# Halving the last adjacency piece block by block in steps 4 to 9, with the x batches' work shifted by a step, in a float32 graph-layer kernel

## The reference

```python
h = jnp.maximum(_layernorm(x, axis=-1), 0.0)      # x: 8192 x 128, float32
support = jnp.matmul(h, W)                        # W: 128 x 128
out = jnp.matmul(adj, support) + b                # adj: 8192 x 8192, float32
x = x + jax.nn.relu(out)
```

## Time and profile before

| | us |
|---|---|
| median of 3 runs | 722.28 (722.16 to 722.79) |
| the profiled execution | 722.6 |
| its span on the core | 720.8 |
| PE busy | 715.5 (99%) |
| DVE busy | 620.4 (86%) |
| ACT busy | 517.0 (72%) |
| POOL busy | 171.5 (24%) |
| DMA | 281.60 MB, mean 391 GB/s |

### The profile page before, as it was taken

One profiled execution on the slowest core, in us unless ns is written; L12 is line 12 of the kernel. 1 busy time (PEld: TensorE's weight loads), 2 busy tenths in 40 slices (PEclk: granted clock), 3 DMA queues, 4 the chain that ended last, 5 costly groups with the idle time before them and its releaser, 6 DMA issues.

```text
span 720.8 us, 7916 instructions
## 1 busy us (share of the span) xinstructions
PE 715.5 (99%) x3125; PEld 586.4 (81%) x3125; DVE 620.4 (86%) x387; ACT 517.0 (72%) x394; POOL 171.5 (24%) x99
## 2 busy tenths in 40 slices
PE   9999999999999999999999999999999999999998
PEld 5788888888888888888888888888888888888886
DVE  5899999999999888988789888878888787888885
ACT  2798988888888867766567677677676676766662
POOL 4445455554444402222011000000000000033213
PEclk9999999999999999999999999999999999999999
DMA  9999999999999999999999999999999999999992
GB/s 352 408 409 407 408 412 415 412 416 415 416 414 416 418 415 412 398 374 402 373 412 392 408 409 389 377 401 383 386 392 373 389 394 387 391 404 397 366 400 85
DMA packets 45109, 281.60 MB, mean 391 GB/s; under 512 B 5136, under 2 KB 5776, under 8 KB 31504
## 3 DMA queue, kind: packets, MB, share of 16 engines
q1 hardware_dynamic: 44496, 280.25, 97.5%
q10 hardware_dynamic: 576, 0.85, 0.4%
HBM read 276.89 MB, written 4.19 MB: 390 GB/s over the span
## 4 chain that ended last, share of the span: by engine, by line
PE 97%; DMA 2%; DVE 0%; ACT 0%; SPq 0%; issue 0%; DVEq 0%
PE banks L558 94%; DMA raw<-adj 2%; PE banks L600 2%; PE banks L592 1%; PE banks L585 0%; PE banks L586 0%; PE banks L584 0%; ACT high L378 0%; SPq L244 0%; DVE x_sb L479 0%; DVE x_sb L487 0%; DVEq L150 0%; DVE warm L491 0%; DVEq L478 0%
## 5 line engine op out<-in xcount | busy, mean ns | idle before, releaser
L516 DVE TENSOR_TENSOR low<-raw,high 128x3072 fp32r<-128x3072 f32 (+2 forms) x255 | 574.7, 2276 | 86.4 <-PE banks L558 64.4
L378 ACT ACTIVATE high<-raw 128x3072 fp32r<-128x3072 f32 (+2 forms) x255 | 483.0, 1903 | 190.3 <-DMA raw<-adj 178.4
L558 PE MATMUL banks<-high,h_high 128*128 128x512 f32 x1012 | 271.6, 390 | 1.1 <-ACT high L378 1.1
L558 PE MATMUL banks<-high,h_low 128*128 128x512 f32 x1012 | 271.0, 389 | 0.0
L558 PE MATMUL banks<-low,h_high 128*128 128x512 f32 x1012 | 267.8, 389 | 0.0
L558 PEld LDWEIGHTS banks<-high,h_high 128*128 128x128 f32 x1012 | 189.8, 188 | 41.8 <-ACT high L378 2.0
L558 PEld LDWEIGHTS banks<-low,h_high 128*128 128x128 f32 x1012 | 189.8, 188 | 39.9 <-DVE low L516 0.4
L558 PEld LDWEIGHTS banks<-high,h_low 128*128 128x128 f32 x1012 | 189.9, 188 | 39.5
L330 POOL TENSOR_SCALAR x_sb<-x_sb,bias 128x512 f32<-128x512 f32 x16 | 49.5, 3095 | 419.3 <-DMA x_sb<-x_blocks 419.3
L321 POOL TENSOR_SCALAR z_sb<-x_sb,neg_mean,rstd 128x128 f32<-128x128 f32 x60 | 89.8, 1510 | 1.6
L306 POOL TENSOR_TENSOR rstd<-var_eps,minus_half 128x4 f32<-128x4 f32 (+2 forms) x17 | 31.6, 1861 | 118.3 <-DVE var_eps L421 109.1
(11 more groups left out here) (34 smaller groups left out, 50.1 us busy)
## 6 DMA issues: line engine op xcount, KB each, us to landing
raw<-adj SPq DMA_DIRECT2D x106, 1536.0 KB, 8.9
raw<-adj SPq DMA_DIRECT2D x82, 768.0 KB, 10.5
raw<-adj SPq DMA_DIRECT2D x69, 512.0 KB, 11.8
x_sb<-x_blocks SPq DMA_DIRECT2D x16, 256.0 KB, 8.6
out_blocks<-x_sb SPq DMA_DIRECT2D x15, 256.0 KB, 9.7
x_sb<-x SPq DMA_DIRECT2D x14, 256.0 KB, 11.9
raw<-adj SPq DMA_DIRECT2D x3, 256.0 KB, 6.9
raw<-adj ACTq DMA_DIRECT2D x1, 256.0 KB, 2.7
```

The costliest lines, as they stand in the source:

```text
L378: nc.scalar.activation(high[:, t % HIGH_SLOTS, cols], raw[:, t % RAW_SLOTS, cols], ACT.Copy).then_inc(high_ready, 1)
L516: nc.vector.tensor_tensor(low[:, t % LOW_SLOTS, cols], raw[:, t % RAW_SLOTS, cols], high[:, t % HIGH_SLOTS, cols].bitcast(F32), ALU.subtra ...
L558: return nc.tensor.matmul(banks[:, FIRST_BANK[g] + c, :], h[:, (t - FIRST_STEP[g]) * DEPTHS[g] + k, :], tile[:, slot, at:at + BANK], start ...
```

## The change

In steps 4 to 9 the last piece (two blocks) is still loaded as one, but ACT, DVE and PE take it as two parts of one block each (`parts_of`), and PE's order is made general for that: high of part n, then low of part n - 1. The load and mean of x batch j come at steps 6, 10, 14, ... (before: 5, 9, 13), the squares at steps 7 and 8, 11 and 12, ... (before 6 and 7), the variance at steps 8, 12, ... (before 7, 11). Batch 3 (tiles 8 to 11) is rectified at step 5 (before: 7); the later batches are rectified at steps 11, 15, ... as before. The split of `h_first` moves from step 9 to step 28. The zero products are 2 of 448 columns (before: 8 of 128); their tile is now a slice of `last_sum`. ACT's first instruction waits for POOL's constant in place of the zeroed tile.

```diff
-WARMING = 8
+HALVED_SINGLY = range(4, 10)
+WARMING, WARM = 2, 448
...
+def parts_of(t):
+    parts = [(i, blocks_of(t, i)) for i in range(len(split_of(t)))]
+    if t in HALVED_SINGLY:
+        i, blocks = parts.pop()
+        parts += [(i, range(c, c + 1)) for c in blocks]
+    return parts
...
 def mean_at(t):
-    return batch_at(t, 1, 3) if t >= 5 else None
+    return batch_at(t, 2, 3) if t >= 6 else None
 def variance_at(t):
-    return batch_at(t, 3, 3) if t >= 7 else None
+    return batch_at(t, 0, 2) if t >= 8 else None
 def rectified_at(t):
-    return 2 if t == 2 else batch_at(t, 3, 2) if t >= 7 else None
+    return {2: 2, 5: 3}.get(t, batch_at(t, 3, 2) if t >= 11 else None)
 def squares_at(t):
-    j = batch_at(t, t % 4, 3) if t >= 6 and t % 4 in (2, 3) else None
-    if j is None:
+    j = batch_at(t, 3, 3) if t % 4 == 3 else batch_at(t, 0, 2)
+    if t < 7 or j is None:
         return None
-    at = BATCHES[j][0] + (t % 4 - 2) * 2
+    at = BATCHES[j][0] + (t % 4 == 0) * 2
...
+        warm = last_sum[:, 0:WARM]
...
-            act.wait_ge(warm_ready, 1)
-            nc.scalar.activation(unread[:, :], warm[:, 0:1], ACT.Square)
+            act.wait_ge(constants_ready, 1)
+            nc.scalar.activation(unread[:, :], minus_half[:, 0:1], ACT.Square)
...
-                for i in range(len(split_of(t))):
-                    cols = columns_of(t, i)
-                    dve.wait_ge(high_ready, halved(t, i))
+                for part, (_, blocks) in enumerate(parts_of(t)):
+                    cols = columns_of(t, blocks)
+                    dve.wait_ge(high_ready, halved(t, part))
...
-                if t == 9:
+                if t == 28:
...
-                nc.tensor.matmul(banks[:, PSUM_BANKS - 1, 0:P], warm[:, :], warm[:, :], start=True, stop=True)
+                nc.tensor.matmul(banks[:, PSUM_BANKS - 1, 0:WARM], warm[:, 0:P], warm[:, :], start=True, stop=True)
...
                 with_high(0)
-                if len(pieces) == 3:
-                    with_high(1)
-                    with_low(0)
-                    with_high(2)
-                    with_low(1)
-                    with_low(2)
-                else:
+                if len(parts) <= 2:
                     with_low(0)
-                    if len(pieces) == 2:
-                        with_high(1)
-                        with_low(1)
+                for part in range(1, len(parts)):
+                    with_high(part)
+                    if len(parts) > 2:
+                        with_low(part - 1)
+                if len(parts) >= 2:
+                    with_low(len(parts) - 1)
```

More of the change, by code:

```diff
@@ L79, in blocks_of, with columns_of @@
     return range(start, start + split_of(t)[i])
-def columns_of(t, i):
-    blocks = blocks_of(t, i)
+def columns_of(t, blocks):
     deep = depth_of(t) * BANK
@@ L88 @@
 HALVED_BEFORE = [0] * (FOUR_PASS + 1)
+def parts_of(t):
[4 more added lines that the diff above has]
+    return parts
 def halved(t, i=None):
     while len(HALVED_BEFORE) <= t:
-        HALVED_BEFORE.append(HALVED_BEFORE[-1] + len(split_of(len(HALVED_BEFORE) - 1)))
-    return HALVED_BEFORE[t] + (len(split_of(t)) if i is None else i + 1)
+        HALVED_BEFORE.append(HALVED_BEFORE[-1] + len(parts_of(len(HALVED_BEFORE) - 1)))
+    return HALVED_BEFORE[t] + (len(parts_of(t)) if i is None else i + 1)
 def landed(t, i):
@@ L170, in gnn_layer @@
         rstd = sb("rstd", [P, TILES])
-        warm = sb("warm", [P, P])
         unread = sb("unread", [P, 1])
@@ L243, in load_piece @@
             def load_piece(t, i):
-                sp.dma_start(raw[:, t % RAW_SLOTS, columns_of(t, i)], adj_piece(t, i)) \
+                sp.dma_start(raw[:, t % RAW_SLOTS, columns_of(t, blocks_of(t, i))], adj_piece(t, i)) \
                   .then_inc(raw_landed[t % RAW_SLOTS][i], 16)
@@ L359, in sum_to_high @@
                                      ACT.Copy).then_inc(sum_high_ready, 1)
-            act.wait_ge(warm_ready, 1)
-            nc.scalar.activation(unread[:, :], warm[:, 0:1], ACT.Square)
-            act.dma_start(raw[:, 0, columns_of(0, 1)], adj_piece(0, 1)).then_inc(raw_landed[0][1], 16)
+            act.wait_ge(constants_ready, 1)
+            nc.scalar.activation(unread[:, :], minus_half[:, 0:1], ACT.Square)
+            act.dma_start(raw[:, 0, columns_of(0, blocks_of(0, 1))], adj_piece(0, 1)).then_inc(raw_landed[0][1], 16)
             for j in (1, 2):
@@ L374, in _ @@
                     act.wait_ge(high_used, t - HIGH_SLOTS - FOUR_PASS + 1)
-                for i in range(len(split_of(t))):
-                    cols = columns_of(t, i)
+                for part, (i, blocks) in enumerate(parts_of(t)):
+                    cols = columns_of(t, blocks)
                     act.wait_ge(raw_landed[t % RAW_SLOTS][i], landed(t, i))
@@ L379, in _ @@
                                          ACT.Copy).then_inc(high_ready, 1)
-                    if i == (0 if t >= NARROW_UNTIL else len(split_of(t)) - 1) and rectified_at(t) is not None:
+                    if part == (0 if t >= NARROW_UNTIL else len(parts_of(t)) - 1) and rectified_at(t) is not None:
                         rectify(rectified_at(t))
@@ L608, in _, with with_high @@
                 depths = range(depth_of(t))
-                pieces = range(len(split_of(t)))
+                parts = parts_of(t)
                 if opens and g >= 2:
                     pe.wait_ge(output_ready, FIRST_BLOCK[g - 1])
-                def with_high(i):
-                    pe.wait_ge(high_ready, halved(t, i))
-                    if i == 0:
+                def with_high(part):
+                    pe.wait_ge(high_ready, halved(t, part))
+                    if part == 0:
                         high_is_there(t)
@@ L618, in with_high @@
                     for k in depths:
-                        for c in blocks_of(t, i):
+                        for c in parts[part][1]:
                             product(t, c, k, h_high, high, t % HIGH_SLOTS, start=opens and k == 0)
-                    if i == 0:
+                    if part == 0:
                         low_is_there(t)
                     for k in depths:
-                        for c in blocks_of(t, i):
+                        for c in parts[part][1]:
                             last = product(t, c, k, h_low, high, t % HIGH_SLOTS)
-                    if i == pieces[-1]:
+                    if part == len(parts) - 1:
@@ L627, in with_high, with with_low @@
                         last.then_inc(high_used, 1)
-                def with_low(i):
-                    pe.wait_ge(low_ready, halved(t, i))
+                def with_low(part):
+                    pe.wait_ge(low_ready, halved(t, part))
                     for k in depths:
-                        for c in blocks_of(t, i):
+                        for c in parts[part][1]:
                             last = product(t, c, k, h_high, low, t % LOW_SLOTS,
                                            stop=closes and k == depth_of(t) - 1)
-                    if i == pieces[-1]:
+                    if part == len(parts) - 1:
```

## The result

The changed kernel takes 726.85 us (median of 12 runs, 723.34 to 729.48); the kernel before, on the same chips, 722.33 (12 runs, 722.15 to 723.26). The ratio is 1.0061, with a 95% interval of 1.0047 to 1.0075: slower by 4.5 us, outside the predicted range. The profiled execution took 726.57 us.

What follows compares the result with a forecast made beforehand. PE, busy 99% of the span, was taken as the bound, so only its waits could be won: 0.30 + 0.29 = 0.59 us off 722.28 gives 721.7 us, range 720.5 to 722.5.

Steps and rivals of the forecast that it cites:

- The variance one step later: Rectifying on ACT waits 0 to 1.4 us for POOL's z at step 15; costed at nothing, upper bound 0.4 us.
- the rival: POOL's chain exceeds 8.7 us in two-piece steps and lengthens each of 9 groups; at 9.1, 725.3 us; chance 0.07.
- Batch 4 behind step 5: Step 5's pieces land 0.7 us earlier, so PE's stall before its third piece falls from 1.22 to 0.5 us.
- block by block: PE starts on step 5's last piece 0.45 us sooner, its stall there falling to about 0.1 us.
- Fewer zero products: PE's stream is 24 instructions shorter, so the instruction packet moves 2.7 us later and step 5 lands undisturbed.
- The packet: An instruction packet on a DMA engine at 28 us, beside step 5's late piece, moves to about 31 us.
- The zero products: At the kernel's start they begin at 1.3 us, last 3.4 us at half the clock and end by 4.7.
- h_first's split: Moving its 0.66 us of DVE from step 9 to 28 wins all 0.29 us of PE's wait, at no cost.
- stall 2: PE's wait of 0.29 us in the four low products beginning at 53.12 us, for DVE's low halves.
- Squares: Gone from step 6, they free 0.77 us of ACT ahead of step 7; rectifying at step 5 costs ACT 0.6.
- The new wall: Step 6's second piece lands late at 33.0 us, so only 0.30 us of PE's stall at step 5 is kept.
- the first rival: The DMA gap does not come back: 720.6 us with no lateness at all, chance 0.12, or 721.3, chance 0.08.

Runs made afterwards that it cites:

- e1: The changed kernel with the x batches' load, mean, squares and variance back at the steps of the kernel before: 722.30 us, ratio 1.0000.
- e2: The kernel before with only the x batches' load, mean, squares and variance one step later, as in the changed kernel: 730.88 us, ratio 1.0117.
- e12: The changed kernel with x's load and the mean back at their earlier steps, squares and variance still late: 733.91 us, ratio 1.0159.
- e7: The changed kernel with three unused one-input sums (1.06 us) on DVE behind the subtractions of every fourth step from 25 on: 724.14 us, ratio 1.0024.
- e9: e5 with one zero product of 448 columns instead of two: 723.01 us, ratio 1.0006.
- e11: e5 with no zero product at all: 722.71 us, ratio 1.0000.
- e5: The changed kernel with only batch 4's load, mean, squares and variance one step later, later batches as before: 722.05 us, ratio 0.9998.
- e6: The changed kernel with one unused one-input sum (0.41 us) on DVE behind the subtractions of every fourth step from 25 on: 727.68 us, ratio 1.0069.
- e10: The changed kernel with the later x batch schedule up to batch 8 and that of the kernel before from step 25 on: 724.81 us, ratio 1.0035.

## Why the prediction was wrong, step by step

**The step that failed is "The variance one step later", costed at nothing with an upper bound of 0.4; the runs showed 5.2 us.** I looked at one place, step 15, in the steps of three pieces, and took the chain of 8.2 us as a property of POOL. At that place the reading held: z is done at 68.84, and the rectifying at 70.71 waits for nothing. In the steps of two pieces the runs showed a loop instead: rectifying, ACT's and DVE's queues, variance, rstd, z, rectifying. In the kernel before, the variance follows a rectifying by 4.15 us (181.23 to 185.38) and z is done at 193.62, 3.36 before the rectifying at 196.98 asks for it. The change puts the variance 7.60 us behind the rectifying (183.42 to 191.02), which takes all of that slack and leaves 16.33 - 7.60 = 8.73 for the chain. That number stood in the prediction, as 8.7, and as a chance of 0.07.

**The term that was mis-sized in the rival** is the chain: 8.2 us from the variance in my rows, 9.9 in the changed kernel (191.02 to 200.94), since z went from 5.4 to 7.0 us. I had read 10.6 once and called 8.2 the usual. It is usual in two ways in the kernel before: z of 7.0 to 7.4 us behind an rstd of 1.01 (at 73.49, 89.52 and 105.53), and, from 122 us on, z of 5.4 behind an rstd of 2.5, because DVE has a gap of some 0.6 us at the right moment while ACT waits for a piece. The loop of the changed kernel has the slow form of both, 2.56 and 7.00. The wait that the change makes closes the door that kept the wait away, so the loop holds itself once it is entered, in every turn that follows. By the rival's own sum, five turns at 1.2 us less the gain give 722.6 + 6.0 - 1.2 = 727.4 against 726.57 measured; the first turn, whose lateness cost PE only 0.2 us, makes up for the 0.8 between them. I had nine turns at 0.4. Mechanism and place are those of the rival. e1, e2 and e12 show the cause, e7 the mechanism of z.

**Right:** *Batch 4 behind step 5*, and the pieces of step 5 block by block: in the kernel after PE doesn't stall there. *Fewer zero products*: ACT's timeline of the kernel after shows the late piece, now in step 6.

```profile
33.84 1.15 ACT L390 ACTIVATE high<-raw 128x512 fp32r<-128x512 f32 x2 [1.18 <-DMA raw<-adj]
```

The packet comes at 30 to 31 us, as said. The zero fill took 0.43 us (0.4 predicted). *The zero products* start at 1.37 us and last 3.22 in the kernel after (1.3 and 3.4 predicted), with weight loads of 0.34 us, while the granted clock reads 1.00 from 0 to 5 us. The first real products lose nothing behind them, by the 190 ns above; e9 and e11 show the slow level behind fewer. *h_first's split*: stall 2 of 0.29 us is gone. *Squares* and the rectifying at step 5: 0.62 us at 29.42, between pieces that ACT awaited anyway.

**The new wall** was right in kind and off by one piece in the changed kernel. There the third piece of step 6 is the late one, and that one is halved block by block, so less comes back: 1.21 us won by step 11 instead of 0.59. In e5 it is the second, as predicted, and 0.74 is won. Why it is the one here and the other there stays open: the packet stands at 30.6 to 30.8 us in both traces.

**Small, as predicted,** is what all of that is worth (no run shows the 1.0 or 1.7 us won that the first rival's 721.3 and 720.6 would take): e1 (without batch 4's move) and e5 (with it) begin step 11 by 0.70 and 0.74 us sooner, and end within 0.4 us of the kernel before, both intervals holding 1.

**Left open.** Why the loop is entered at one turn in one kernel and later in another, and why rstd takes 1.0 us in one turn and 2.5 or over 4 in another: in e2 the entry falls on an rstd of 4.11 us (141.85), in the changed kernel it does not. The wide spread of the changed kernel's runs (723.3 to 729.5) would fit entries at different groups, which I argue and have not shown. Why the instruction packet at 28 us has a late piece beside it (2.78 us between two pieces) and the one at 60 us has none: no run here shows the DMA engines one by one. No version tried beats both kernels by more than the runs can tell; e5 (722.05) is the nearest.

## What to carry to other kernels

Before moving a producer later, close the loop. Add up everything that stands in the queues between the point where the consumer's engine waits and the point where the producer's input is made, add the producer's chain, and compare the sum with the period: the move may take no more than the difference. Take the producer's duration at its longest in the trace and find what made it short elsewhere, since a move can take that away. For the GpSimd chain of this kernel it was not VectorE's load that counted but how long its two-input subtractions followed each other without a break: 1.06 us of something else at the right place gave back 2.7 of the 4.5 us lost.

## What the runs showed of the hardware

- A 128x128 float32 TENSOR_SCALAR on GpSimd takes 0.45 us beside an idle VectorE or a one-input instruction, and 0.9 to 4.2 us beside back-to-back two-input subtractions in the changed kernel (up to 5.2 in e6, at 248.35); in the rows shown it ends 0.24 to 0.33 us after they do. Most boundaries between them let no tile through (30 against 7 in the changed kernel), some do: in the changed kernel at 179.00, in e12 at 134.48, where the tile had begun 0.07 us ahead of a subtraction (132.43). What decides it isn't settled. A one-input instruction of 0.41 us lets one tile through (e6), 1.06 us three (e7).
- rstd, a 128x4 power on GpSimd, takes 1.0 us (109.29 in the changed kernel) or 2.0 to 2.6 (2.05 at 60.82, 2.56 at 191.27), at times 4.1 to 4.2 (e2 at 141.85, and the earlier trace rows) and once 7.45 (e10, 139.79), there with four subtractions in a row beside it.
- The granted clock reads 1.00 from 5 to 10 us in e11, while the weight loads take 338 ns against 190: at the start of this kernel the durations tell the level, and the column doesn't. The window, with its columns as in the earlier trace rows:

```profile
5.00:10.00 5.00, 4.69 (x6) 2.07 (x7) 3.88 (x25) 0.00 (x0) 1.08 (x2) 1.00 1.03 412
```
